# Row-wise squared sums, a transpose and interleaved seam products in a gated linear-attention layer

## The reference, cut to what matters

```python
q = _causal_dwconv(_silu(x @ Wq), conv_q_w)      # the same for k and v; 16 heads of 128
q = q * cos + rot_half(q) * sin                  # rotary positions, the same for k
q = q / jnp.maximum(jnp.linalg.norm(q, axis=-1, keepdims=True), 1e-12)
k = k / jnp.maximum(jnp.linalg.norm(k, axis=-1, keepdims=True), 1e-12)
for s in range(K):                               # four lags
    attn = jnp.einsum('bshd,bshd->bsh', q, k_s) * scale
    out = out + (attn * jax.nn.sigmoid(a_s * b))[..., None] * v_s
out = out * rms * norm_w * _silu(z)
return out @ Wout
```

## Time and profile before

| | us |
|---|---|
| timed runs, median of 3 | 1207.07 |
| lowest and highest | 1204.34, 1210.94 |
| the profiled execution's own time | 1207.07 |
| its span in the profile | 1205.3 |
| TensorE busy in the span | 1060.0 |
| VectorE, ScalarE, GpSimd busy | 752.9, 549.1, 278.9 |
| mean granted TensorE clock | 0.914 of full |

### The profile page before, as it was taken

One profiled execution on the slowest core, in us unless ns is written; L12 is line 12 of the kernel. 1 busy time (PEld: TensorE's weight loads), 2 busy tenths in 40 slices (PEclk: granted clock), 3 DMA queues, 4 the chain that ended last, 5 costly groups with the idle time before them and its releaser, 6 DMA issues.

```text
span 1205.3 us, 16895 instructions
## 1 busy us (share of the span) xinstructions
PE 1060.0 (88%) x5843; PEld 833.0 (69%) x5843; DVE 752.9 (62%) x1259; ACT 549.1 (46%) x1051; POOL 278.9 (23%) x243
## 2 busy tenths in 40 slices
PE   6799999999999969946986999999997987639986
PEld 4588888889888954422434889998897443338876
DVE  1398788778878828963125787778776155513344
ACT  1176676667666738930112655555553022213320
POOL 0023322332233220003002112211210005146660
PEclk9699999999899978977997999999998998769997
DMA  7156766676768561050000111111100101058944
GB/s 256 19 146 145 146 131 163 148 144 129 162 150 177 137 162 32 1 166 26 1 0 27 54 53 52 42 37 52 52 0 0 66 1 69 30 171 275 273 158 180
DMA packets 73017, 121.54 MB, mean 101 GB/s; under 512 B 24771, under 2 KB 50062, under 8 KB 72208
## 3 DMA queue, kind: packets, MB, share of 16 engines
q1 hardware_dynamic: 60944, 86.91, 23.8%
q0 software_dynamic: 12032, 34.11, 14.7%
HBM read 70.31 MB, written 38.08 MB: 90 GB/s over the span
## 4 chain that ended last, share of the span: by engine, by line
PE 63%; DVE 16%; ACT 9%; issue 6%; POOL 2%; DMA 2%; ACTq 0%; DVEq 0%; POOLq 0%; SPq 0%
PE psum L574 8%; PE psum L576 7%; PE psum L575 7%; PE psum L808 5%; PE psum L922 4%; PE psum L597 4%; PE psum L884 4%; PE psum L781 3%; DVE arena L1259 2%; PE psum L689 2%; ACT arena L1042 2%; PE psum L629 2%; PE psum L932 2%; DVE arena L1350 2%; PE psum L727 2%
## 5 line engine op out<-in xcount | busy, mean ns | idle before, releaser
L1259 DVE SCALAR_TENSOR_TENSOR arena<-arena,par_in 128x1024 f32<-128x1024 f32 x144 | 183.3, 1283 | 19.2 <-ACT arena L999 7.8
L574 PE MATMUL psum<-lut_w_r,arena_r 128*128 128x512 f32 x320 | 140.4, 439 | 19.9 <-POOL arena_r L1675 10.1
L575 PE MATMUL psum<-lut_w_r,arena_r 128*128 128x512 f32 x320 | 135.3, 423 | 0.0
L576 PE MATMUL psum<-lut_w_r,arena_r 128*128 128x512 f32 x320 | 134.4, 420 | 0.0
L1659 POOL DMA_DIRECT2D arena<-arena x64 | 53.8, 983 | 242.7 <-DVE arena L1271 242.5
L1090 ACT ACTIVATE arena<-psum,small 128x256 f32<-128x256 f32 x128 | 59.4, 474 | 85.8 <-DVE small L1392 85.7
L989 ACT ACTIVATE arena<-psum 128x1024 f32<-128x1024 f32 x48 | 49.3, 1027 | 99.8 <-PE psum L576 99.8
L574 PEld LDWEIGHTS psum<-lut_w_r,arena_r 128*128 128x128 f32 x320 | 64.8, 202 | 34.9 <-issue 13.6
L574 PE MATMUL psum<-arena_r 128*128 128x256 f32 x256 | 77.7, 304 | 1.5 <-DVE arena_r L1417 1.5
L576 PEld LDWEIGHTS psum<-lut_w_r,arena_r 128*128 128x128 f32 x320 | 66.2, 207 | 16.5
L575 PEld LDWEIGHTS psum<-lut_w_r,arena_r 128*128 128x128 f32 x320 | 66.5, 208 | 13.0
(11 more groups left out here) (216 smaller groups left out, 2312.0 us busy)
## 6 DMA issues: line engine op xcount, KB each, us to landing
arena<-arena POOLq DMA_DIRECT2D x64, 256.0 KB, 5.6
arena<-in_w_moe SPq DMA_DIRECT2D x33, 384.0 KB, 3.8
slot_rows<-nowhere SPq DMA_DIRECT2D x16, 576.0 KB, 4.8
arena<-slot_rows SPq DMA_DIRECT2D x32, 288.0 KB, 3.9
arena<-bands SPq DMA_DIRECT2D x16, 528.0 KB, 4.0
arena<-in_w_qkvz SPq DMA_DIRECT2D x16, 512.0 KB, 3.8
sq_rows<-arena POOLq DMA_DIRECT2D x16, 512.0 KB, 5.8
arena<-in_qkv_codes SPq DMA_DIRECT2D x16, 384.0 KB, 3.2
```

The costliest lines, as they stand in the source:

```text
L574: nc.tensor.matmul(dst, w_l, x_h, start=start, stop=False, skip_group_check=True)
L575: nc.tensor.matmul(dst, w_h, x_l, start=False, stop=False, skip_group_check=True)
L576: return nc.tensor.matmul(dst, w_h, x_h, start=False, stop=stop, skip_group_check=True)
L1259: nc.vector.scalar_tensor_tensor(by_batch(dst), by_batch(u[s])[:, :, j:j + S], par_in[:, bass.ds(M_CW + (w * H + h) * TAPS + j, 1)], by_ba ...
```

## The change

There are four edits:

- The squared sums: now `select(n)` is stationary (16 columns) and the block of squares is moving (128 columns). The eight blocks of q (n = 0 to 7) and the eight of k (n = 8 to 15) add up into one block of 16 rows and 128 columns in bank 7.
- Back to one column per tile: VectorE copies this block into the new tile `rows_sb` (its other rows are zeroed once at the start), TensorE transposes `rows_sb` as a whole into columns 128 to 255 of bank 7, and VectorE clamps 16 columns of that into `ssq_s`. The transpose stands between the projections of v and z on TensorE. On VectorE the copy stands where the clamp stood, and the clamp now between the convolutions of q and of k, with a wait for the transpose ahead of it.
- The product of A and v: the four seam products (3 stationary columns each), which stood behind all eight tile products, now stand each behind the tile product that it adds to; each tile product starts its own accumulation.
- The arena grows by 128 columns, so that some tiles start 128 columns further, and GpSimd zeroes `rows_sb` at the start.

```diff
@@ -156,14 +156,14 @@
 
         UW = B * (S + PAD)
         (uq, uk, uv, cq, ck, cv0, cv1, qr, kr, sqq, sqk, sz0, sz1, A,
-         gm0, gm1, v_tok, gates, swq, swk, wh0, wh1) = carve(
+         rows_sb, gm0, gm1, v_tok, gates, swq, swk, wh0, wh1) = carve(
             UW, UW, UW, T, T, T, T, T + TAPS, T, T, T, T, T, BAND,
-            BAND, BAND, T, H * NT * TAPS, T, T, 4 * KC * P, 4 * KC * P)
+            P, BAND, BAND, T, H * NT * TAPS, T, T, 4 * KC * P, 4 * KC * P)
         gm = [gm0, gm1]
         u, c_ = {"q": uq, "k": uk, "v": uv}, {"q": cq, "k": ck}
         sw, rot, sqr = {"q": swq, "k": swk}, {"q": qr[:, 0:T], "k": kr}, {"q": sqq, "k": sqk}
         cv, sz, wh = [cv0, cv1], [sz0, sz1], [wh0, wh1]
-        at_w = 3 * UW + 13 * T + TAPS + 3 * BAND + H * NT * TAPS
+        at_w = 3 * UW + 13 * T + TAPS + 3 * BAND + P + H * NT * TAPS
         wl0, _, wl1, _, w_hi0, w_hi1 = carve(QKV, KC * P, QKV, KC * P, QKV, QKV, base=at_w, of=arena_r)
         w_lo, w_hi = [wl0, wl1], [w_hi0, w_hi1]
         wmod = [G[:, 0:KC * 6 * D], G[:, KC * 6 * D:2 * KC * 6 * D]]
@@ -173,7 +173,7 @@
         ln_c, ln_sq, ln_b, rb, gsb, hsb0, hsb1, lv0, lv1, lb0, lb1 = carve(
             KC * T, KC * T, T, T, T, T, T, (PAIRS - 1) * LC, (PAIRS - 1) * LC, LC, LC)
         lut_v, lut_b0 = [lv0, lv1], [lb0.bitcast(I32), lb1.bitcast(I32)]
-        (wout,) = carve(H * D, base=3 * UW + 11 * T + TAPS + 3 * BAND + H * NT * TAPS)
+        (wout,) = carve(H * D, base=3 * UW + 11 * T + TAPS + 3 * BAND + P + H * NT * TAPS)
         hsb = [hsb0, hsb1]
 
         QK = 2 * KC * P
@@ -626,8 +626,8 @@
                 def squared_sums(j, s):
                     for i in range(NT):
                         n = j * NT + i
-                        m = nc.tensor.matmul(bank(7)[:, n:n + 1], sqr[s][:, i * P:i * P + P], ones[:, 0:1],
-                                             start=True, stop=True, skip_group_check=True)
+                        m = nc.tensor.matmul(bank(7)[0:2 * NT, 0:P], select(n), sqr[s][:, i * P:i * P + P],
+                                             start=(n == 0), stop=(n == 2 * NT - 1), skip_group_check=True)
                     return m
 
                 if 2 in st:
@@ -652,6 +652,9 @@
                     for n in range(2):
                         i = project0(slot(0), 2, n)
                     i.then_inc(sg("a0_v"), 1)
+                if 2 in st:
+                    pe.wait_ge(sg("a0_rows_sb"), h)
+                    nc.tensor.transpose(bank(7)[:, P:2 * P], rows_sb, ident).then_inc(sg("a0_ssqT"), 1)
                 if 1 in st:
                     pe.wait_ge(sg("a0_silu_k"), h + 1)
                     for t in range(NT):
@@ -686,12 +689,13 @@
                     pe.wait_ge(sg("a0_v_tok"), h)
                     pe.wait_ge(sg("a0_silu_z"), evens(h))
                     for i in range(NT):
-                        nc.tensor.matmul(slot(1)[:, i * P:i * P + P], A[:, i * WIDE:i * WIDE + P], v_tok[:, i * P:i * P + P],
-                                         start=(i % 4 == 0), stop=(i % 2 == 0), skip_group_check=True)
-                    for i in range(1, NT, 2):
-                        c = (i - 1) * WIDE + P
-                        m = nc.tensor.matmul(slot(1)[0:PAD, i * P:i * P + P], A[:, c:c + PAD], v_tok[:, (i - 1) * P:i * P],
-                                             start=False, stop=True, skip_group_check=True)
+                        o = slot(1)[:, i * P:i * P + P]
+                        m = nc.tensor.matmul(o, A[:, i * WIDE:i * WIDE + P], v_tok[:, i * P:i * P + P], start=True, stop=(i % 2 == 0),
+                                             skip_group_check=True)
+                        if i % 2:
+                            c = (i - 1) * WIDE + P
+                            m = nc.tensor.matmul(o[0:PAD, :], A[:, c:c + PAD], v_tok[:, (i - 1) * P:i * P], start=False,
+                                                 stop=True, skip_group_check=True)
                     m.then_inc(sg("a0_o"), 1)
 
             pe.wait_ge(sg("in_lo"), KC)
@@ -1277,10 +1281,16 @@
                 if 2 in st:
                     dve.wait_ge(sg("a0_ssq"), h)
                     if since(h, 2):
+                        dve.wait_ge(sg("a0_ssqT"), h - 1)
+                    nc.vector.tensor_copy(rows_sb[0:2 * NT, :], bank(7)[0:2 * NT, 0:P]).then_inc(sg("a0_rows_sb"), 1)
+                if 1 in st:
+                    conv(0, "q", cq)
+                if 2 in st:
+                    dve.wait_ge(sg("a0_ssqT"), h)
+                    if since(h, 2):
                         dve.wait_ge(sg("a0_rqk"), h - 1)
-                    nc.vector.tensor_scalar(ssq_s, bank(7)[:, 0:2 * NT], 1e-24, None, ALU.max).then_inc(sg("a0_ssq_s"), 1)
-                if 1 in st:
-                    conv(0, "q", cq)
+                    nc.vector.tensor_scalar(ssq_s, bank(7)[:, P:P + 2 * NT], 1e-24, None, ALU.max).then_inc(sg("a0_ssq_s"), 1)
+                if 1 in st:
                     conv(1, "k", ck)
                 if 4 in st:
                     lower0(h + 1, 1 - par)
@@ -1635,7 +1645,9 @@
             pool.wait_ge(*norm("n0", "out"))
             for s in "qkv":
                 nc.gpsimd.memset(by_batch(u[s])[:, :, 0:PAD], 0.0)
-            nc.gpsimd.memset(qr[:, T:T + TAPS], 0.0).then_inc(sg("pool_set"), 1)
+            nc.gpsimd.memset(qr[:, T:T + TAPS], 0.0)
+            i = nc.gpsimd.memset(rows_sb, 0.0)
+            i.then_inc(sg("pool_set"), 1)
 
             pool.wait_ge(sg("sq_nil"), 48)
 
```

More of the change, by code:

```diff
@@ L1279, in turn @@
                     if since(h, 2):
-                        dve.wait_ge(sg("a0_rqk"), h - 1)
-                    nc.vector.tensor_scalar(ssq_s, bank(7)[:, 0:2 * NT], 1e-24, None, ALU.max).then_inc(sg("a0_ssq_s"), 1)
+                        dve.wait_ge(sg("a0_ssqT"), h - 1)
+                    nc.vector.tensor_copy(rows_sb[0:2 * NT, :], bank(7)[0:2 * NT, 0:P]).then_inc(sg("a0_rows_sb"), 1)
                 if 1 in st:
                     conv(0, "q", cq)
+                if 2 in st:
+                    dve.wait_ge(sg("a0_ssqT"), h)
+                    if since(h, 2):
+                        dve.wait_ge(sg("a0_rqk"), h - 1)
+                    nc.vector.tensor_scalar(ssq_s, bank(7)[:, P:P + 2 * NT], 1e-24, None, ALU.max).then_inc(sg("a0_ssq_s"), 1)
+                if 1 in st:
                     conv(1, "k", ck)
```

## The result

| | before | changed |
|---|---|---|
| median of 20 runs each, us | 1208.90 | 1216.49 |
| lowest and highest, us | 1201.27, 1216.81 | 1211.36, 1223.05 |
| span of the profiled execution, us | 1205.3 | 1220.1 |

The ratio is 1.0059, 95% interval 1.0039 to 1.0081: slower by 5 to 10 us. The prediction said 1206.3 us and no change clear of noise, with 1213 as its upper bound. Of the 10.2 us between the forecast and the median, 1.8 lie in the starting point (1208.90 us here, 1207.07 there).

A forecast was written before the change was run, and what follows sets the result against it. TensorE was taken to set the pace in layer 0's attention, slowed by half clock. Twelve turns at -0.40 us gave -4.8, the other turns +4.0: -0.8 from 1207.07, so 1206.3 us, range 1196 to 1213.

The forecast's parts named there:

- the clock costs 1.54 us per turn, twelve times: 18.5 us: q's projection in turns 2 to 13: half clock makes it 4.42 us against 2.88; the change removes this.
- a change of width costs 0.09 us each way ... +0.62 us: Product of A and v: interleaved seams add six changes of stationary width per head on TensorE, +0.62 us.
- the transpose and its wait ... +0.52 us: VectorE waits for the transpose before the clamp, runs 1.0 us late and delays ScalarE's square of k: +0.52 us.
- The +0.05 us for k's sums: k's squared sums on TensorE: change of width and uncovered load behind them, less what is saved: +0.05 us.
- Turn 15, +1.4 us: No q projection there; k's convolution starts later behind the transpose, on the chain to the rotary DMA: +1.4 us.
- The first (free interleaving): Product of A and v: interleaved seams cost nothing, 16 x 0.62 = 9.9 us fall away, 1196.4 us; chance 0.13.
- The second (the clock falls all the same): q's projection or the stretch after: half clock remains, 1.54 us each, 1224.8 us if in all turns; chance 0.15.
- The third: Some falls return when the turn's length changes; the twelve turns give nothing, the rest costs 4.0: 1211.1 us; chance 0.10.
- turns 2 to 13: Twelve full turns with a fall: each changes by -1.54 + 0.52 + 0.62 = -0.40 us, together -4.8 us.
- turn 14: Full turn already at full clock, so it only pays: +0.52 + 0.62 = +1.1 us.

The follow-up runs named there:

- the sums wide: Kernel before with the squared sums of q and k moving 128 columns of ones in place of one, nothing else: 1193.24 us, ratio 0.9836.
- the seams alone: Kernel before with only the product of A and v edited, its seam products interleaved as in the change: 1231.25 us, ratio 1.0133.
- full-width seams: Changed kernel, interleaved, with seam products at 128 stationary columns in place of 3 (attention output differs): 1207.67 us, ratio 0.9995.
- q's sums wide: Kernel before with 128 moving columns of ones in the squared sums of q alone, those of k keeping one: ratio 0.9857.

## Why the prediction failed

**The full turn.** By differences of measured turns: 22.33 us with the sums wide (kernel before, no falls); +0.08 for 16-row sums and an early transpose (22.41); +0.45 for the transpose behind v (22.86); +0.87 for the interleaving (23.73). The sum of the added terms is 1.40 us, and the removed fall is worth 1.56.

- *Step "the clock costs 1.54 us per turn, twelve times: 18.5 us".* The price of a fall was right (1.56), and that the new sums keep the clock up too. **The count failed.** I took twelve falls from one execution for a property of the kernel. On average over seven there are 8.3, so the edit gives back 12.9 us, 5.6 less than I booked. The first trace alone could not show this: its one full turn without a fall, turn 14, has none in any of the seven. A second profile would not have shown it either (twelve falls again), the third did.
- *Step "a change of width costs 0.09 us each way ... +0.62 us".* The mechanism was right and **the term was mis-sized: 0.87 us**. The change costs 0.09 each way as read; what I put at 0.02, the uncovered load behind a return, costs 0.10, three times per head. The earlier trace rows had only the return to sums with one moving column, where the excess is 0.02; the row after the first 128-column matmul of L727 would have shown it (0.53 us to the next start where 0.43 is the step). Over the twelve turns 2 to 13 this is 12 x 0.25 = 3.0 us.
- *Step "the transpose and its wait ... +0.52 us".* Right: VectorE 0.64 us idle, ScalarE 0.43, and 0.45 + 0.08 on the turn. The +0.05 us for k's sums was worked out but not added into the sum.
- *Turn 15, +1.4 us.* The wait was there and something else took it back. From the product of turn 14 to that of turn 15 it took 21.47 us where it was 19.27; the late transpose makes 1.1 of it, with the interleaving (21.47 against 20.35 with an early one) and without (20.61 against 19.48). From the scores of turn 15 to those of turn 16, the stretch that ends with the rotary DMA, the late transpose makes 1.1 us without the interleaving (18.61 to 19.69) and 1.6 with it (16.97 to 18.54). But with the interleaved 3-column seams that DMA lands sooner after its issue: 7.98 us in the changed kernel and 6.61 with the seams alone, where it took 9.26 before and 9.13 with full-width seams. So the two nearly cancel: 18.54 us after, 18.56 before. Why the DMA is shorter there no run shows.
- *Rivals.* The first (free interleaving) is refuted by the steps and by the full-width seams; its price counts sixteen products of A and v, where the sum has fifteen. The second (the clock falls all the same) is refuted by three profiles of the changed kernel with no fall in turns 1 to 15. The third named falls that come and go with the turn's length, but in the changed kernel, where there are none; they come and go in the kernel before.

The averages over seven and three profiles, cut from product to product as in the earlier trace rows, show where the forecast of the change (-0.8 us) and the measured loops (+7.4) part:

| stretch | forecast, us | measured, us |
|---|---|---|
| up to the product of turn 1 | +0.2 | +0.1 |
| turns 2 to 13 | -4.8 | +3.9 |
| turn 14 | +1.1 | +1.0 |
| from there to the output projection | +2.7 | +2.3 |

The miss lies in turns 2 to 13, and the two sizes account for it: -4.8 + 5.6 + 3.0 = +3.8. The last line came near by luck: turns 15 and 16 together gave +0.3 us (+2.2 and -1.9), and the stretch from the last product on gave +2.0. That product itself is 1.9 us longer on average, 0.9 of it what the seams cost at full clock; the rest goes with its half clock, which the forecast did not have.

Why q's narrow sums bring a fall in some turns and not in others of the same kernel was not settled. In all 58 falls half clock begins 2.6 to 3.5 us after the first of these sums; those of the turns 2 to 13 that have none have the same sums and the same pause behind them. So the narrow sums are needed for a fall here, but do not suffice. The number goes with the execution, and not with the length of the start: with 53.8 us there were twelve falls once and five twice.

Three of the versions tried are faster than before by about 1.5%, and their intervals overlap: both sums wide (0.9836), q's sums wide (0.9857), and the early transpose without interleaving (0.9854). The first two are edits of one line and need no transpose, no tile and no wait.

## What to carry to other kernels

Here a matmul with one moving column and a full-width stationary operand took TensorE as long as one with 128 (1.95 us for sixteen instructions either way); where such a group brings the clock down, widen the moving operand into columns that are overwritten anyway before the sums are restructured. Group matmuls of one stationary width: every excursion to a narrow one and back costs about 0.29 us here. A loss that hangs on the granted clock is to be counted in several executions: here the number of falls per run went from 5 to 12 while their place and price stayed.

## What was not expected of the hardware

- The number of falls in one and the same kernel: 5, 5, 5, 7, 12, 12, 12 in seven profiles, always behind q's sums, 1.5 to 1.6 us each. It alone moves the loop by 11 us, more than the measured difference between the kernels.
- The return to the full width costs twice, 0.09 us for the change and 0.10 for a weight load that does not start ahead; with 0.09 on the way out a round trip costs 0.29 us. The Trainium skill (TensorEngine Tiling (Array Packing), Key Properties) says that a change of the tiling mode drains TensorE. It does not say whether fewer stationary columns are such a change; the pauses in this trace would fit it, and no run here shows the mode.
- The Trainium skill (TensorE: Matmul & The Clock Gate, HAM oscillation) ties falls to pauses of TensorE. This case's traces do not bear that out for these falls. The pause ahead of one was 0.16 us, while eight falls of the seams-only kernel stand behind k's sums with no pause at all, and the changed kernel pauses for 0.43 us at the same place (23.29 us busy of 23.72) and has none. The falls vanished when the moving operand became wider, with the projection following as late as before (2.00 us from the first of the sums to L574, 2.01 in the earlier trace rows).
